# Four edits to a chain of expert and scan blocks: ranking by halves, scan weights requested a stage earlier, a changed order in the gated scan, and a first sequence with an order of its own

## The chip, the cores and the metric

One NeuronCore of one Trainium2 chip runs the whole program in one launch. The metric is the time of that launch on the device in microseconds (us). Names of engines in the profile: PE is TensorE, DVE is VectorE, ACT is ScalarE, POOL is GpSimd, and SP is SyncE, which here only issues DMAs.

## What is computed

The input is x of shape [8, 1024, 128] in f32: 8 sequences of 1024 tokens, 128 features. Six blocks follow each other, each reading a layer-normalised x and adding to x. Cut to what matters, the reference is:

```python
x = x + 0.5 * L0_ffn(layernorm(x))    # m0: 8 experts, the best two by logits, gated
x = x + L0_attn(layernorm(x))         # s0: gated scan
x = x + 0.5 * L0_ffn(layernorm(x))    # m1: as m0
x = x + 0.5 * L1_ffn(layernorm(x))    # m2: 8 experts, the best two by probabilities, capacity
x = x + L1_attn(layernorm(x))         # s1: selective scan
x = x + 0.5 * L1_ffn(layernorm(x))    # m3: as m2

# L0_ffn: logits = xn @ Wg + bg; the two largest, softmax over the two
#   y = (silu(xn @ W1a + b1a) * (xn @ W1b + b1b)) @ W2 + b2, summed by weight
# L1_ffn: probs = softmax(x @ router_w.T); the two largest, rank within the expert,
#   those beyond the capacity dropped; y = silu(x @ w1) @ w2, plus x
# L0_attn: xc, z = split(x @ W_in); u = silu(conv4(xc)); dt_raw, B = split(u @ W_x)
#   dt = clip(softplus(dt_raw @ W_dt + b_dt), 1e-4, 1); ub = u * (B @ W_Bp)
#   h[t] = h[t-1] * (1 - dt[t]) + ub[t]; y = (h + D * u) * silu(z); y @ W_out
# L1_attn: u = silu(conv4(x) + b); dt, B, C by head from u; delta = softplus(dt @ dtw + b)
#   s[t] = s[t-1] * exp(delta * A) + delta * u * B[t], for 16 states; y = sum(s * C) ...
```

## The kernel before

**Blocks.** The six blocks run one behind the other, each as one or more groups of engine programs with semaphores of its own; x (`x_res`, [128, 64, 128]: 64 tiles of 128 tokens) stays in SBUF.

**Experts (`moe`).** A block begins with ranking. The 64 tiles go in 16 groups of four (`NG` = 16): VectorE makes statistics (`statistics`, `spreads`, `scales`), ScalarE takes the root (`root`), normalises (`normalise`) and copies the rows turned by TensorE (`copy_out`); TensorE multiplies them with the gate (`logits`) into one PSUM tensor `lps` of 64 x 8 numbers per partition. When all 16 groups are there, VectorE works on [128, 64, 8] at a time: in m0 and m1 it adds the gate's bias (L337), in m2 and m3 it copies (L341), takes the maximum and the difference, has ScalarE make the exponential (L535), and divides. Then for the best and the second-best expert it takes the maximum, marks what is below, adds the index of the expert and takes the least (L354 to L362); `chosen` (L364) is what TensorE counts from. There follow ranks and runs, 16 groups of marks by which TensorE finds for each row of the sorted list its token (L495), and the block map (`bmap`, L442 to L449): for each of the 73 blocks of 128 rows the expert whose run it lies in. Before, every partition computes it for all 73 blocks: it compares 73 x 8 numbers (m0, m1) or 73 x 32 (m2, m3, where there are `S` = 4 rounds of runs) and sums them, and where there are rounds it takes 8 off three times. `source` (L456) is the list of tokens. SyncE, once it has issued the expert weights (`loads`), waits for the rows that it stored. The expert loop then runs over 71 blocks per kind of expert; the change doesn't touch it. Between blocks of the program the engines meet.

**Gated scan (`gated_scan`, L892 on).** The loop is over v, at each v of which the engines work on several sequences: TensorE projects sequence v+1 (`project_in`, `project_z`, `project_low`, `project_wide`), projects out v-1 (`project_out`) and turns the rows of v+2; ScalarE scales the fetched rows of v+3 (L1195), normalises v+2 (L1143), makes u by silu (L1163, L1179), and copies z (L1173) and xp (L1206); VectorE convolves half 0 of v+1 (L1263; half 1 is convolved on TensorE by four taps, L1067), adds the output of v-1 (L1239), makes statistics of v+2, scans v (L1278) and reads the wide projections (L1303, L1306). Eight PSUM banks go round in the order of one list, `order` (L955), so TensorE's order of blocks and the list are one. At its start SyncE issues the 16 loads of the weights (L989), then the fetches of rows (L1009); the engines wait for all loads.

**Selective scan (`selective_scan`, L1324 on).** For each of 8 sequences there are 2 halves x 16 states, 256 steps in all of 128 x 1024: ScalarE makes dA (L1694), POOL dBu (L1558), VectorE scans (L1873) and multiplies with C (L1880), TensorE sums. The work for sequence t = s + 1 is put in 32 slots i within the 32 steps of s; for t = 0 the slots run without steps, s = -1. Lists of slots say when each engine's `conv`, silu, `xd`, `dt`, exponential and logarithm stand. `soften` (L1536) is four operations on POOL: from the pieces of the softplus they make delta, and du = delta * u. SyncE stores the rows of B and C and loads them spread over the partitions.

## Time and profile before

| | us |
|---|---|
| median of 3 runs | 3280.31 |
| lowest, highest | 3279.01, 3280.53 |
| the execution that was profiled | 3282.22 |
| its span in the trace | 3279.4 |
| ranking of m0, m1, m2, m3 | 105.4, 103.5, 162.6, 121.6 |
| expert loops of m0, m1, m2, m3 | 410.4, 406.5, 277.3, 376.4 |
| gated scan | 285.9 |
| selective scan | 1017.5 |

The stages are cut at 12.3, 117.7, 528.1, 814.0, 917.5, 1324.0, 1486.6, 1763.9, 2781.4, 2903.0 and 3279.4 us of the span. In a timeline each row gives the start and the length in us, the engine, the line of the kernel, what is written from what, how many instructions of a kind the row gathers (its length then is that of all of them), and in brackets how long the engine was idle before it and which engine's or queue's event ended that. A window's row gives for each engine the busy time and the number of instructions in it, then TensorE's granted clock (1.00 is full speed) and the busy share of the DMA engines.

### The profile page before, as it was taken

The numbers are of one execution on the slowest core, as the hardware profiler recorded it, in microseconds if no ns is written. First come the engines' busy times: TensorE is split into PE (matmuls) and PEld (weight loads), VectorE is DVE, ScalarE is ACT, GpSimd is POOL, SyncE is SP. The second block draws the span as 40 slices with busy tenths as digits, with TensorE's granted clock in tenths as the row PEclk, the third lists the DMA queues.
The fourth block names the chain that finished last, engine by engine and source line by source line (L and its number), as shares of the span: only waits on it lengthen the run. The fifth ranks groups of instructions, "written<-read, shape, count | busy, mean of one in ns | idle before, by whom it ended". The sixth has DMA issues, their size and how long they took to land. (4 is left out here: it accounts for less than half of the span.)

```text
span 3279.4 us, 43901 instructions
## 1 busy us (share of the span) xinstructions
PE 2580.4 (79%) x12400; PEld 1850.5 (56%) x12400; DVE 2222.7 (68%) x3998; ACT 1575.7 (48%) x2668; POOL 2018.0 (62%) x1643
## 2 busy tenths in 40 slices
PE   5799994996689999348996678788877875579782
PEld 4599993443579999327995233333332322559672
DVE  5656663786766666683332699999999998653333
ACT  4433333884533333333333667567577662443330
POOL 0377771232057776305772789999999784335776
PEclk9999997998599999569998899999999999589997
DMA  6111112100411111422332689889888886312333
GB/s 180 32 48 48 46 48 56 39 26 1 135 37 48 46 47 40 134 72 61 87 87 43 243 291 310 278 296 305 285 291 301 288 300 207 103 40 76 92 90 85
DMA packets 287326, 429.78 MB, mean 131 GB/s; under 512 B 59196, under 2 KB 196799, under 8 KB 287200
## 3 DMA queue, kind: packets, MB, share of 16 engines
q1 hardware_dynamic: 251744, 357.54, 33.1%
q0 software_dynamic: 35456, 70.86, 9.3%
q8 instruction: 42, 0.69, 0.1%
q14 instruction: 84, 0.69, 0.1%
HBM read 367.71 MB, written 62.39 MB: 131 GB/s over the span
## 5 line engine op out<-in xcount | busy, mean ns | idle before, releaser
L683 POOL DMA_INDIRECT m_rows<-rows_in,m_source x568 | 554.0, 975 | 588.6 <-SPq L580 222.2
L1593 PE MATMUL s_y_ps<-s_prod,ident 128*128 128x512 f32 x1024 | 522.0, 634 | 214.3 <-DVE s_prod L1880 214.3
L1558 POOL TENSOR_TENSOR s_dBu<-s_du,s_B_row 128x1024 f32<-128x1024 f32 x256 | 602.4, 2359 | 84.6 <-DVE s_dA L1873 71.1
L1873 DVE TENSOR_TENSOR_SCAN s_dA<-s_dA,s_dBu 128x1024 f32<-128x1024 f32 x256 | 585.6, 2287 | 44.3 <-POOL s_dBu L1558 44.3
L721 PE MATMUL m_A_ps<-m_rowsT,m_own 128*128 128x256 f32 x2272 | 569.0, 383 | 2.1 <-ACT m_rowsT L763 1.1
L737 PE MATMUL m_Y_ps<-m_own,m_hid 128*128 128x128 f32 x4544 | 556.1, 276 | 3.6 <-issue 3.6
L737 PEld LDWEIGHTS m_Y_ps<-m_own,m_hid 128*128 128x128 f32 x4544 | 531.4, 192 | 5.7 <-issue 5.6
L1593 PEld LDWEIGHTS s_y_ps<-s_prod,ident 128*128 128x128 f32 x1024 | 180.9, 195 | 523.3 <-DVE s_prod L1880 325.9
L773 ACT ACTIVATE m_act_a<-m_A_ps,m_own 128x256 f32<-128x256 f32 x568 | 238.5, 471 | 434.7 <-PE m_A_ps L721 318.9
L721 PEld LDWEIGHTS m_A_ps<-m_rowsT,m_own 128*128 128x128 f32 x2272 | 414.9, 193 | 48.8 <-ACT m_rowsT L763 1.9
L1694 ACT ACTIVATE s_dA<-s_delta,s_decay 128x1024 f32<-128x1024 f32 x256 | 286.0, 1118 | 311.0 <-DVE s_prod L1880 306.2
L690 POOL DMA_INDIRECT rows_by_token<-m_y_sb,m_target x284 | 308.8, 1087 | 121.9 <-issue 90.6
L822 DVE SCALAR_TENSOR_TENSOR m_hid<-m_B_ps,m_own,m_act_a 128x256 f32<-128x256 f32 x568 | 247.2, 477 | 200.2 <-ACT m_act_a L773 183.5
L778 ACT ACTIVATE m_hid<-m_A_ps 128x512 f32<-128x512 f32 x284 | 169.7, 598 | 335.9 <-PE m_A_ps L721 335.9
L1880 DVE TENSOR_TENSOR s_prod<-s_dA,s_C_row 128x1024 f32<-128x1024 f32 x256 | 313.2, 1223 | 10.1 <-issue 1.4
L727 PE MATMUL m_B_ps<-m_rowsT,m_own 128*128 128x256 f32 x1136 | 293.4, 381 | 0.0
L836 DVE COPY m_y_sb<-m_Y_ps 128x256 f32<-128x256 f32 x142 | 60.3, 425 | 328.3 <-PE m_Y_ps L737 328.3
L727 PEld LDWEIGHTS m_B_ps<-m_rowsT,m_own 128*128 128x128 f32 x1136 | 217.3, 191 | 30.0
L805 DVE COPY m_own<-m_packs 128x1032 f32 (+1 forms) x284 | 172.7, 608 | 71.5 <-PE m_A_ps L721 47.2
L643 POOL DMA_INDIRECT m_mine<-rows_out,get x176 | 169.2, 961 | 59.1 <-issue 40.8
L715 PE MATMUL m_T_ps<-ident,m_rows 128*128 128x128 f32 x568 | 112.5, 280 | 81.2 <-DMA m_rows<-rows_in,m_source 81.2
L495 PE MATMUL m_src<-m_coded,m_is_low 128*128 128x284 bf16 x512 | 82.2, 307 | 101.3 <-ACT m_coded L538 101.3
(241 smaller groups left out, 3543.9 us busy)
## 6 DMA issues: line engine op xcount, KB each, us to landing
s_B_row<-s_bc_rows SPq DMA_DIRECT2D x256, 512.0 KB, 5.7
s_C_row<-s_bc_rows SPq DMA_DIRECT2D x256, 512.0 KB, 6.0
rows_out<-m_y_sb SPq DMA_DIRECT2D x142, 128.0 KB
rows_in<-m_xs SPq DMA_DIRECT2D x64, 256.0 KB, 2.3
m_rows<-rows_in,m_source POOLq DMA_INDIRECT x568
s_got<-rows_by_token SPq DMA_DIRECT2D x16, 512.0 KB, 5.0
m_got<-rows_by_token SPq DMA_DIRECT2D x32, 256.0 KB, 3.9
rows_by_token<-m_y_sb,m_target POOLq DMA_INDIRECT x284
```

The costliest lines, as they stand in the source:

```text
L683: pool.indirect_dma_start(rows[:, b % AHEAD, r, :], None, c.rows_in, bass.IndirectOffsetOnAxis(source[:, 2 * b + r:2 * b + r + 1], 0)).the ...
L690: pool.indirect_dma_start(c.rows_by_token, bass.IndirectOffsetOnAxis(target[:, 2 * b + r:2 * b + r + 1], 0), y_sb[:, b % AHEAD, r, :], Non ...
L721: ins = nc.tensor.matmul(A_ps[h][:, j, :], own[:, slot, W1A + f * P:W1A + (f + 1) * P], rowsT[:, slot, :], start=True, stop=True)
L727: ins = nc.tensor.matmul(B_ps[h][:, j, :], own[:, slot, W1B + f * P:W1B + (f + 1) * P], rowsT[:, slot, :], start=True, stop=True)
L737: ins = nc.tensor.matmul(Y_ps[slot][:, r, :], hid[:, slot, f, at(r, P)], own[:, slot, W2 + f * D:W2 + (f + 1) * D], start=(f == 0), stop=( ...
L773: ins = nc.scalar.activation(act_a[:, h, j, :], A_ps[h][:, j, :], ACT.Silu, bias=own[:, slot, B1A + f:B1A + f + 1])
L822: ins = nc.vector.scalar_tensor_tensor(out=hid[:, slot, f, :], in0=B_ps[h][:, j, :], scalar=own[:, slot, B1B + f:B1B + f + 1], in1=act_a[: ...
L1558: nc.gpsimd.tensor_tensor(dBu[q % RING][:, :], du[s % 2][:, h, :], B_row[q % RING][:, :], ALU.mult).then_inc(dBu_ready, 1)
L1593: ins = nc.tensor.matmul(y_ps[:, at(cc, 512)], c.ident[:, :], prod[q % 2][:, at(cc, 512)], start=(n == 0), stop=(n == NS - 1))
L1694: nc.scalar.activation(dA[q % 2][:, :], delta[s % 2][:, h, :], ACT.Exp, scale=decay[:, h, n:n + 1]).then_inc(dA_ready, 1)
L1873: nc.vector.tensor_tensor_scan(dA[q % 2][:, :], dA[q % 2][:, :], dBu[q % RING][:, :], 0.0, ALU.mult, ALU.add).then_inc(scanned, 1)
L1880: nc.vector.tensor_tensor(prod[q % 2][:, :], dA[q % 2][:, :], C_row[q % RING][:, :], ALU.mult).then_inc(prod_ready, 1)
```

## The change

**Ranking.** `lps` becomes two PSUM tensors, and the operations on [128, 64, 8] become two of [128, 32, 8]. The first half runs when eight of 16 groups have their logits. In m2 and m3 its copy, maximum and difference stand ahead of the statistics of group 14, and its exponential ahead of the normalising of that group.

```diff
+                def softmax(part, step):
+                    ts = at(part, NT // 2)
+                    if step == 0:
+                        dve.wait_ge(logits_done, (part + 1) * NG // 2)
+                        link(nc.vector.tensor_copy(L[:, ts, :], lps3[part]))
+                        link(nc.vector.tensor_reduce(m[0][:, ts], L[:, ts, :], AX.X, ALU.max))
+                        nc.vector.tensor_tensor(t8[:, ts, :], L[:, ts, :], over_experts(m[0][:, ts]), ALU.subtract).then_inc(logits_shifted, 1)
+                    else:
+                        dve.wait_ge(exp_done, part + 1)
+                        link(nc.vector.tensor_reduce(ind[:, ts], u8[:, ts, :], AX.X, ALU.add))
+                        link(nc.vector.reciprocal(rank[:, ts], ind[:, ts]))
+                        link(nc.vector.tensor_tensor(L[:, ts, :], u8[:, ts, :], over_experts(rank[:, ts]), ALU.mult))
+
+                def best_two(part):
+                    ts = at(part, NT // 2)
+                    for k in range(2):
+                        link(nc.vector.tensor_reduce(m[k][:, ts], L[:, ts, :], AX.X, ALU.max))
+                        link(nc.vector.tensor_tensor(t8[:, ts, :], L[:, ts, :], over_experts(m[k][:, ts]), ALU.is_lt))
+                        link(nc.vector.scalar_tensor_tensor(out=t8[:, ts, :], in0=t8[:, ts, :], scalar=float(E),
+                                                            in1=c.expert_id[:, ts, :], op0=ALU.mult, op1=ALU.add))
+                        link(nc.vector.tensor_reduce(ind[:, ts], t8[:, ts, :], AX.X, ALU.min))
+                        link(nc.vector.tensor_tensor(oh[k][:, ts, :], c.expert_id[:, ts, :], over_experts(ind[:, ts]), ALU.is_equal))
+                        if k == 0:
+                            link(nc.vector.scalar_tensor_tensor(out=L[:, ts, :], in0=oh[0][:, ts, :], scalar=-3e38,
+                                                                in1=L[:, ts, :], op0=ALU.mult, op1=ALU.add))
+
                 for g in range(NG):
                     if rows_before:
                         add_rows(g)
                     if g % 2 == 0 and g > 0:
                         scales(g // 2 - 1)
+                    if g == NG - 2 and not gated:
+                        softmax(0, 0)
                     statistics(g)
                     if g % 2 == 1:
                         spreads(g // 2)
...
+                for part in range(2):
+                    if gated:
+                        dve.wait_ge(logits_done, (part + 1) * NG // 2)
+                        link(nc.vector.tensor_tensor(L[:, at(part, NT // 2), :], lps3[part],
+                                                     gate_b[:, :].unsqueeze(1).to_broadcast([P, NT // 2, E]), ALU.add))
+                    else:
+                        if part == 1:
+                            softmax(1, 0)
+                        softmax(part, 1)
+                    best_two(part)
```

The same operations on the whole tensors, which stood behind the wait for all 16 groups, are gone.

**Block map.** `block_row` is one number per partition (128 times the partition), so partition p computes for block p only; a diagonal matrix of the result is multiplied by ones on TensorE, and the row copied out of `tot_ps`.

```diff
+                link(nc.vector.tensor_scalar(passed[:, :], run_end[:, :, :].rearrange("p i e -> p (i e)"), c.block_row[:, 0:1], None, ALU.is_le))
+                link(nc.vector.tensor_reduce(bmap[:, :], passed[:, :], AX.X, ALU.add))
+                link(nc.vector.tensor_copy(bmap_i[:, :], bmap[:, :]))
+                link(nc.vector.tensor_scalar(bmap_i[:, :], bmap_i[:, :], E - 1, None, ALU.bitwise_and))
+                link(nc.vector.tensor_copy(bmap[:, :], bmap_i[:, :]))
+                nc.vector.tensor_scalar(spread_map[:, :], c.ident[:, :], bmap[:, 0:1], None, ALU.mult).then_inc(map_ready, 1)
...
                 link(nc.vector.tensor_tensor(source[:, :], code, second, ALU.add))
+                dve.wait_ge(map_spread, 1)
+                link(nc.vector.tensor_copy(block_pack[:, :], tot_ps[:, 0:NBLK + 2]))
...
+                pe.wait_ge(map_ready, 1)
+                nc.tensor.matmul(tot_ps[:, 0:P], c.ones_bf[:, :], spread_map[:, :], start=True, stop=True).then_inc(map_spread, 1)
```

The exponential on ScalarE (lines as in the changed kernel), of the block m2:

```diff
+                def exponentials(part):
+                    act.wait_ge(logits_shifted, part + 1)
+                    nc.scalar.activation(u8[:, at(part, NT // 2), :], t8[:, at(part, NT // 2), :], ACT.Exp).then_inc(exp_done, 1)
+
...
+                        exponentials(0)
                     normalise(g)
                     if g > 0:
                         copy_out(g - 1)
                 copy_out(NG - 1)
-                act.wait_ge(logits_shifted, 1)
                 if gated:
```

ScalarE's order in block m2 between the root of the last pair of groups (L504 before, L521 now) and the exponential (L535, L542). Names: `m_xs` normalised rows, `m_xcT` turned rows, `m_u` exponentials. Before:

```order
L504 ACTIVATE m_spread<-m_spread 128x8
L512 ACTIVATE m_xs<-x_res,m_shift,m_rstd 128x128 x4
L521 COPY m_xcT<-m_tps 128x512
L512 ACTIVATE m_xs<-x_res,m_shift,m_rstd 128x128 x4
L521 COPY m_xcT<-m_tps 128x512 x2
L535 ACT_TABLE_LOAD
L535 ACTIVATE m_u<-m_t 128x512
```

Now:

```order
L521 ACTIVATE m_spread<-m_spread 128x8
L542 ACT_TABLE_LOAD
L542 ACTIVATE m_u<-m_t 128x256
L529 ACTIVATE m_xs<-x_res,m_shift,m_rstd 128x128 x4
L538 COPY m_xcT<-m_tps 128x512
L529 ACTIVATE m_xs<-x_res,m_shift,m_rstd 128x128 x4
L538 COPY m_xcT<-m_tps 128x512 x2
L542 ACTIVATE m_u<-m_t 128x256
```

The table load and half of the exponential now stand ahead of the last eight rows of `m_xs`; the second half stays behind the copies, without a load.

**Weights.** Each scan's weight tensors are allocated outside both stages, so that they live through m0 (m2) as well. POOL clears two of them at the start of that block's ranking, and SyncE issues the 16 loads there.

```diff
+                if ahead is not None:
+                    ahead.request(sp)
...
+    def request(sp):
+        def load(dst, src, **kw):
+            sp.dma_start(dst, src, **kw).then_inc(weights.loaded, 16)
+        load(weights.w_in[:, :], w["w_in"])
+        load(weights.tap_rows[:, :, :], w["taps"].rearrange("(a k) i -> a k i", a=1).to_broadcast([P, CONV, INNER]))
...
+        for h in range(HALVES):
+            load(weights.w_x[:, h, :, :], w["w_x"][at(h, P), :].unsqueeze(1).to_broadcast([P, COPIES, PAIR]))
+        sp.wait_ge(weights.zeroed, 2)
+        for r in range(COPIES):
+            load(weights.w_dt[r * PAIR:r * PAIR + PAIR // 2, :], w["w_dt"])
+            load(weights.w_b[r * PAIR + PAIR // 2:r * PAIR + PAIR, :], w["w_b"])
+    weights.clear, weights.request = clear, request
```

The loads themselves are those removed from the scans' programs; SyncE's program of the gated scan now begins with the fetch of rows.

**Gated scan.** TensorE's blocks and the list of banks change order, `y` gets a second buffer, and VectorE adds the output behind the scan.

```diff
         order = []
         for v in range(-3, SEQS + 1):
-            for s, uses in ((v + 1, (("in", range(N_DVE)),)), (v - 1, (("out", range(2)),)),
-                            (v + 1, (("in", range(N_DVE, HALVES * HC)), ("z", range(HALVES * HC)), ("low", range(HC)),
-                                     ("wide", range(HALVES * HC)))),
+            for s, uses in ((v + 1, (("in", range(HALVES * HC)), ("z", range(HALVES * HC)), ("low", range(HC)))),
+                            (v - 1, (("out", range(2)),)), (v + 1, (("wide", range(HALVES * HC)),)),
                             (v + 2, (("turned", range(2)),)), (v + 1, (("wide", range(HALVES * HC, 2 * HALVES * HC)),)),
                             (v + 3, (("sum", range(4)),))):
...
                 if has(v + 1):
-                    project_in(v + 1, range(N_DVE))
+                    project_in(v + 1, range(HALVES * HC))
+                    project_z(v + 1)
+                    project_low(v + 1)
                 if has(v - 1):
                     project_out(v - 1)
                 if has(v + 1):
-                    project_in(v + 1, range(N_DVE, HALVES * HC))
-                    project_z(v + 1)
-                    project_low(v + 1)
                     project_wide(v + 1, 0)
                 if has(v + 2):
...
-                if s > 0:
+                if s > 1:
                     for g in range(2):
-                        Use("out", s - 1, g).read(dve)
+                        Use("out", s - 2, g).read(dve)
...
                 if has(v + 1):
                     convolve(v + 1)
-                if has(v - 1):
-                    add_out(v - 1)
                 if has(v + 2):
                     statistics(v + 2)
                 if has(v):
                     scan(v)
+                if has(v - 1):
+                    add_out(v - 1)
                 if has(v + 1):
                     widened(v + 1)
```

TensorE's order of one period of the gated scan; names: `s_w_in` with `s_xnT` the projections in (L1071, L1162) and z (L1079, L1170), `s_w_conv` the four taps, `s_w_out` the projection out, `s_w_x` low, `s_w_dt` and `s_w_b` wide, `ident` the turned rows. Before:

```order
L1071 MATMUL s_bank<-s_xnT,s_w_in 128x512 x2
L1054 MATMUL s_bank<-s_w_out,s_y 128x128 x16
L1067 MATMUL s_bank<-s_xnT,s_w_conv 128x512 x8
L1079 MATMUL s_bank<-s_xnT,s_w_in 128x512 x4
L1098 MATMUL s_bank<-s_u,s_w_x 128x512 x4
L1108 MATMUL s_bank<-s_xp,s_w_dt 128x512 x4
L1089 MATMUL s_bank<-ident,s_xn 128x128 x8
```

Now:

```order
L1162 MATMUL s_bank<-s_xnT,s_w_in 128x512 x2
L1158 MATMUL s_bank<-s_xnT,s_w_conv 128x512 x8
L1170 MATMUL s_bank<-s_xnT,s_w_in 128x512 x4
L1189 MATMUL s_bank<-s_u,s_w_x 128x512 x4
L1145 MATMUL s_bank<-s_w_out,s_y 128x128 x16
L1199 MATMUL s_bank<-s_xp,s_w_dt 128x512 x4
L1180 MATMUL s_bank<-ident,s_xn 128x128 x8
```

The sixteen matmuls of the projection out went from behind the first two of `s_w_in` to between low and the wide dt.

**Selective scan, first sequence.** Half 0 goes through ahead of half 1, on TensorE and ScalarE; VectorE softens half 0 in place of POOL; B and C rows of half 0 are stored and loaded from slot 16, those of half 1 from slot 26. du of a half waits for u of that half alone.

```diff
+                if t == 0:
+                    for h in range(HALVES):
+                        order += [(role, 0, h * HC + cc) for role in ("conv", "xd", "dt") for cc in range(HC)]
+                else:
+                    order += [("conv", t, k) for k in range(3)] + [("xd", t, 0), ("xd", t, 1), ("conv", t, 3)]
+                    order += [("dt", t, 0), ("dt", t, 1), ("xd", t, 2), ("xd", t, 3), ("dt", t, 2), ("dt", t, 3)]
             if EARLY <= t + 1 < SEQS:
...
+                if t == 0:
+                    if i == 16:
+                        store_bc(0, (0,))
+                        sp.wait_ge(bc_stored, 16)
                         for q in range(RING):
                             load_B(q)
                             load_C(q)
-                if s == -1 and i == ALLN - 1:
-                    for q in range(RING, RING + 2):
-                        load_B(q)
-            sp.wait_ge(loaded, LOADS)
+                    if i == 26:
...
+                if s == -1:
+                    XD_AT, DT_AT = (13, 14, 21, 22), (15, 16, 23, 24)
+                    CONV_AT = (9, 10, 11, 12, 17, 18, 19, 20)
...
+                if s == -1:
+                    CONV_AT, SILU_AT, XD_AT, DT_AT = (11, 12, 21, 22), (13, 23), (14, 15, 24, 25), (16, 17, 27, 28)
+                    EXP_AT, LOG_AT, ROUNDED_AT = (18, 29), 19, 20
                 if 0 <= s < SEQS:
...
+                if s == -1 and 26 <= i < 30:
+                    soften_on(dve, nc.vector, 0, 0, i - 26)
```

ScalarE's order there; `s_u` is u, `s_xd` the low projection, `s_e` and `s_delta` the two forms of dt. Before:

```order
L1726 ACTIVATE s_u<-s_bank,s_conv_b 128x512 x2
L1743 ACT_TABLE_LOAD
L1743 ACTIVATE s_u<-s_u 128x1024
L1726 ACTIVATE s_u<-s_bank,s_conv_b 128x512
L1752 COPY s_xd<-s_bank 96x512 x2
L1726 ACTIVATE s_u<-s_bank,s_conv_b 128x512
L1743 ACTIVATE s_u<-s_u 128x1024
L1760 ACTIVATE s_e<-s_bank,s_dt_b 128x512
L1761 ACTIVATE s_delta<-s_bank,s_dt_b 128x512
```

Now:

```order
L1806 ACTIVATE s_u<-s_bank,s_conv_b 128x512 x2
L1823 ACT_TABLE_LOAD
L1823 ACTIVATE s_u<-s_u 128x1024
L1832 COPY s_xd<-s_bank 96x512 x2
L1840 ACTIVATE s_e<-s_bank,s_dt_b 128x512
L1841 ACTIVATE s_delta<-s_bank,s_dt_b 128x512
L1840 ACTIVATE s_e<-s_bank,s_dt_b 128x512
L1841 ACTIVATE s_delta<-s_bank,s_dt_b 128x512
L1846 ACT_TABLE_LOAD
L1846 ACTIVATE s_e<-s_e 128x1024
```

The copies of xd and the dt of half 0 now stand directly behind its silu, with its exponential's table load next; conv and silu of half 1 went behind them.

## Rows read from the trace of the kernel before

**Rows 1.** Busy time of each engine in two stages (columns as named)

```profile
1324.00:1486.60 162.60, 63.03 (x322) 51.78 (x322) 131.40 (x420) 58.60 (x108) 31.60 (x64) 0.59 0.36 104
...
1763.90:2781.40 1017.50, 775.46 (x1856) 314.94 (x1856) 940.00 (x714) 631.18 (x745) 843.94 (x431) 0.94 0.81 275
```

**Rows 2.** The same view, one period of the gated scan

```profile
644.70:673.57 28.87, 27.02 (x93) 14.17 (x92) 25.12 (x42) 23.87 (x45) 10.19 (x4) 1.00 0.14 37
```

**Rows 3.** Timeline, gated scan's start: start, length, engine, line, operation, count, [idle before]

```profile
528.09 0.34 SPq L989 DMA_DIRECT2D s_w_in<-in_L_attn_W_in  x1
...
537.52 1.05 SPq L1009 DMA_DIRECT2D s_got<-rows_by_token  x2
...
544.71 0.37 ACT L1195 ACTIVATE s_bank<-s_got,weight 128x128 f32<-128x128 f32 x1 [32.93 <-DMA s_got<-rows_by_token]
```

**Rows 4.** Timeline, VectorE, selective scan's start and its first scan

```profile
1775.31 1.43 DVE L1902 TENSOR_TENSOR s_w_conv<-s_e 128x256 f32<-128x256 f32 x4 [15.72 <-DMA s_w_dt<-in_dt_proj_T]
...
1830.39 2.30 DVE L1873 TENSOR_TENSOR_SCAN s_dA<-s_dA,s_dBu 128x1024 f32<-128x1024 f32 x1 [44.31 <-POOL s_dBu L1558]
```

**Rows 5.** Timeline, VectorE, ranking of block m0

```profile
61.16 0.69 DVE L337 TENSOR_TENSOR m_L<-m_lps,m_gate_b 128x512 f32<-128x512 f32 x1 [8.66 <-PE m_lps L476]
...
69.85 0.69 DVE L364 TENSOR_TENSOR m_chosen<-m_oh 128x512 bf16<-128x512 f32 x1
```

**Rows 6.** Groups of instructions by line and shape: 256 elements on VectorE

```profile
L832 DVE TENSOR_TENSOR m_y_sb<-m_Y_ps,m_own_b 128x256 f32<-128x256 f32 x142 | 60.3, 425 | 106.5 <-PE m_Y_ps L737 106.5
```

**Rows 7.** Timeline, end of ranking in block m1

```profile
912.57 1.19 PE L495 MATMUL m_src<-m_coded,m_is_low 128*128 128x284 bf16 x8 [0.73 <-ACT m_coded L538]
...
914.15 0.31 DVE L452 TENSOR_SCALAR m_found<-m_src 128x142 f32<-128x142 f32 x1
```

**Rows 8.** Timeline, first sequence of the selective scan, ScalarE and POOL

```profile
1796.90 1.28 ACT L1743 ACT_TABLE_LOAD   x1
1798.19 1.06 ACT L1743 ACTIVATE s_u<-s_u 128x1024 f32<-128x1024 f32 x1
...
1806.69 0.67 ACT L1760 ACTIVATE s_e<-s_bank,s_dt_b 128x512 f32<-128x512 f32 x1
...
1818.18 2.34 POOL L1537 TENSOR_TENSOR s_e<-s_e 128x1024 f32<-128x1024 f32 x1 [36.42 <-ACT s_e L1777]
```

**Rows 9.** Timeline, ranking of block m2, ScalarE and VectorE

```profile
1402.63 1.65 ACT L512 ACTIVATE m_xs<-x_res,m_shift,m_rstd 128x128 f32<-128x128 f32 x4 [0.62 <-DVE m_own_shift L319]
...
1411.26 0.69 DVE L341 COPY m_L<-m_lps 128x512 f32<-128x512 f32 x1 [8.66 <-PE m_lps L476]
...
1424.08 0.69 DVE L364 TENSOR_TENSOR m_chosen<-m_oh 128x512 bf16<-128x512 f32 x1
```

**Rows 10.** Timeline, ScalarE, ranking of block m3

```profile
2819.89 1.65 ACT L512 ACTIVATE m_xs<-x_res,m_shift,m_rstd 128x128 f32<-128x128 f32 x4 [0.62 <-DVE m_own_shift L319]
```

**Rows 11.** Timeline, VectorE, block map of block m2

```profile
1476.90 2.59 DVE L442 TENSOR_TENSOR m_passed<-block_row,m_run_end 128x2336 f32<-128x2336 f32 x1
...
1483.90 0.31 DVE L452 TENSOR_SCALAR m_found<-m_src 128x142 f32<-128x142 f32 x1
```

**Rows 12.** Timeline, one period of the gated scan, TensorE and ScalarE

```profile
660.30 3.59 PE L1098 MATMUL s_bank<-s_u,s_w_x 128*128 128x512 f32 x8
665.75 3.67 PE L1108 MATMUL s_bank<-s_xp,s_w_dt 128*128 128x512 f32 x8 [1.85 <-ACT s_xp L1206]
...
657.61 1.07 ACT L1163 ACTIVATE s_u<-s_bank 128x512 f32<-128x512 f32 x2
...
661.52 3.18 ACT L1143 ACTIVATE s_xn<-x_res,s_shift,s_rstd 128x128 f32<-128x128 f32 x8 [0.42 <-POOL s_shift L1024]
664.61 1.04 ACT L1206 COPY s_xp<-s_bank 128x512 f32<-128x512 f32 x2
```

**Rows 13.** Timeline, TensorE, an earlier period of the gated scan

```profile
601.82 5.40 PE L1098 MATMUL s_bank<-s_u,s_w_x 128*128 128x512 f32 x8 [1.86 <-ACTq L1166]
```

**Rows 14.** The page's costliest groups: 1024 elements on VectorE

```profile
L1880 DVE TENSOR_TENSOR s_prod<-s_dA,s_C_row 128x1024 f32<-128x1024 f32 x256 | 313.2, 1223 | 10.1 <-issue 1.4
```

356 lines of the change are left out of this document (181 added, 175 removed).

## The prediction

> **What bounds the kernel now.** I read the page first, then the busy times by stage, then timelines around each edited place. The execution that was profiled took 3282.22 us, of which 3279.4 are its span. The median of the runs shown is 3280.31, 1.9 less, so whatever I work out for the profiled execution is laid on the median with that shift. No engine bounds the whole: in the selective scan VectorE is busy 940.0 of 1017.5 us [rows 1], in the expert loops TensorE is, and in between lie stretches where the engines wait for each other once per stage. The change touches three such stretches (ranking, the start of each scan, the first sequence of the selective scan) and one loop, the gated scan, where TensorE is busy 27.02 of each 28.87 us, VectorE 25.12 and ScalarE 23.87 [rows 2]. So each edit is read at its place, for what ends last there.
>
> **Weights a stage ahead.** In the gated scan SyncE issues 16 loads before the first rows; the first is issued at 528.09 and the fetch of rows follows at 537.52. ScalarE starts to scale those rows at 544.71, 7.2 us after the fetch [rows 3]. With the loads gone the fetch stands at 528.1, ScalarE starts at 535.3: **-9.4 us**. VectorE's products of the convolution weights and its scalings then run at once, under the fetch's 7 us. In the selective scan the stage begins at 1763.9 and VectorE and ScalarE wait for the last load until 1775.31 [rows 1, 4]; nothing else is waited for, since x is in SBUF: **-11.4 us**. The loads don't vanish: 16 issues of together 9 us go to SyncE behind that routing block's own weight loads, ahead of its waits for the stored rows, and their cover is the ranking that runs then (SyncE has nothing to store or fetch until it ends; the stage of m2 lasts 162.6 us with its DMA engines busy 36% [rows 1]). If the cover were gone, 9 us would come back in each.
>
> **Ranking by halves, gated blocks (m0, m1).** From the last logits VectorE runs 12 operations of 512 elements, 61.16 to 69.85, a pitch of 0.724 and 0.69 for one; before them it sat idle 8.66 us [rows 5]. A 256-element operation takes 0.42 [rows 6]; with the same 0.035 between two I take 0.46. Behind the last logits now stand 12 half operations, 5.5 us instead of 8.69: -3.2 each. The other half (5.5) fits in the idle of 8.66. Two blocks: **-6.4**. The block map's two operations of 584 elements (0.8 each) make way for six small ones, a matmul and a copy; the source table that follows starts at 914.15, when TensorE's last group of marks (912.57 plus 1.19) ends [rows 7], so the saving stops at that matmul: 0.
>
> **The same in m2 and m3.** There the first half begins before the last statistics: three half operations on VectorE (3 x 0.46 = 1.4 us), then on ScalarE the exponential with its table load (1.28 as in [rows 8], plus 0.4) before the last two groups are normalised. In m2 VectorE runs without a gap up to ScalarE's normalising at 1402.63 [rows 9] and hands on its 1.4 us; with ScalarE's share, less the 0.62 that ScalarE waits there, I get 2.5 us for the last logits, so the copy of the logits moves from 1411.26 to 1413.7. Behind it: 1.4 (copy, maximum, difference), 0.4 (exponential), 1.3 (sum, reciprocal, product), 11 x 0.46 = 5.1, to 1421.9, against 1424.08 [rows 9]: -2.2. In m3 VectorE waits for ScalarE there, its 1.4 us fit, and only ScalarE's 1.7 less its wait of 0.62 counts, 1.1 us [rows 10]: -3.7. The block map is 2336 elements wide here: its first operation takes 2.59 and the whole, from 1476.90 to the next table at 1483.90, 7.0 us [rows 11]. In its place come six operations on 32, 1 and 128 elements and a copy of 73, each at or below the 0.31 that 142 elements take [rows 7]; at 0.22 to 0.28 they are 1.6 us: **-5.4 each**, since VectorE alone sets this tail and the matmul that spreads the map runs under the source table's five operations. Both blocks: -2.2 - 3.7 - 10.8 = **-16.7**.
>
> A table load in this trace is followed by its activation after 1.29 us (1796.90, then 1798.19) [rows 8]. The Trainium skill ("ScalarE: Activation LUTs", What ACT_TABLE_LOAD costs) has about 1380 ns of drain on top for each switch; here that would be 1.4 more in m2, in m3 and for the extra switch in the selective scan, and a total of about -42 instead of -46. The row shows none of it, and I leave it out.
>
> **The gated scan's loop.** TensorE's order changes from in, out, in (four taps), z, low, wide to in, in, z, low, out, wide. Its only gap is 1.85 us before the wide dt at 665.75, waiting for ScalarE's copy of xp (664.61 plus 1.04) [rows 12]. Behind z the low projection needs ScalarE's u, which ends at 657.61 + 1.07 = 658.68 after ScalarE has run from the turned copy without a gap. Now low could start at 658.8 and not 660.30: low 3.43, out 3.57, wide dt at 665.8, where it stood at 665.75. So the gap moves from before the wide dt to before low (some 2 us) and the period stays: **0 for some six periods**. The ends between which this lies: ScalarE's own round leaves 0.42 (before 661.52 [rows 12]) and 0.16, so if out did not stand in the way the gain would be 0.6 a period, -3.5; if the whole gap closed, -11. The other end is TensorE's clock: a low block of eight that takes 3.59 took 5.40 at 601.82, behind a gap of 1.86, in this scan [rows 12, 13]. If each new gap brought that, 6 x 1.8 = +11. I take 0, because the arithmetic of the long round leaves it at +0.02, and the old gap was as long as the new one. The output's addition on VectorE moves behind the scan, where it fits before the wide dt; the second buffer of y keeps it off the scan.
>
> **First sequence of the selective scan.** From silu of half 0 (ends 1799.25) the old chain runs over ScalarE, then four POOL operations of 2.34 from 1818.18, then dBu, to the first scan at 1830.39 [rows 4, 8]. Now half 0 runs through alone: xd and dt on TensorE and ScalarE to 1804.9, exponential, logarithm and rounding with two tables 6.9 (to 1811.8), softening on VectorE in four operations of 1.22 (the shape of [rows 14]) to 1816.9, dBu 2.4 more. What ends last then is ScalarE: before the first decay it must also do all of half 1 (conv, a table and silu, xd, dt, a table and exponential). By rows that is, from 1799.25 on, 12 evacuations of xd and dt at a pitch of 0.57, 2 of conv at 0.6, 4 tables at 1.29, 6 activations of 1024 elements at 1.06 and the rounding at 1.15 [rows 8], together 20.7 us, and I count 4.6 of waiting for TensorE (its xd and dt blocks of 1.1 to 1.8 us stand between ScalarE's): the decay starts at 1824.6, the first scan at 1825.7, -4.7. With TensorE at its lower clock behind the new gaps, half as much again or more as in [rows 13], it is 1830 or so. **Taken -2.5, bounds -4.7 and +0.5.** The 256 steps behind it keep their pitch of 3.46, which is VectorE's scan and product.
>
> **Sum.** -9.4 - 11.4 - 6.4 - 16.7 + 0 - 2.5 = **-46.4**; 3282.2 - 46.4 = 3235.8 profiled, and 3280.3 - 46.4 = **3234** as a median.
>
> **The rivals.**
> (a) The gated scan's periods lengthen by the clock. For it: 601.82, and a routing stage with gaps that is granted 0.59 of the clock [rows 1, 13]; against it: in the period shown the clock was 1.00 although it held a gap of 1.85 [rows 2, 12]. +11: 3245.
> (b) The periods shorten, because the out block fills time and the output's addition no longer stands ahead of the statistics. For it: 0.58 of slack on ScalarE; against it: out stands between low and the wide dt. -3.5 to -11: 3223 to 3230.
> (c) The first sequence gives nothing, or the halves in m2 and m3 give only what the block map does: +2.5 or +5.9, 3237 to 3240.
> (d) The change does not do what it says: the loads, issued among a routing block's traffic, hold up its rows, or the first halves run late and stand before the last statistics. Losing one scan's load and half of the ranking gives 3254.
> (e) **Slower.** TensorE at half clock through the whole run from the new gap: low, out and wide dt, 3.43 + 3.57 + 3.51 = 10.5 us of work that ends last, in each period. That costs +10.5 x 6 = 63, and the total is 3297, +17. It decides from 8.8 us lost per period on (53 us), since below that the 46 saved and the 6.6 of the bound hold. The row of 601.82 shows 1.8 lost, not 8.8.
>
> **How the numbers follow.** The forecast with (c), which ends within its bounds: 0.66, of which 0.10 for (c). (a) 0.15, (b) 0.12, (d) 0.06, (e) 0.01. The forecast's own bounds are 3229 to 3241. To leave out no more than 2 in 10 the range takes (a) and most of (b): **3222 to 3250**. About 0.2% (6.6 us) is what a measurement can tell from no change. Cases (a) to (d) all end more than that below, though (d) could be heavier than I price it: faster 0.98, same 0.01, slower 0.01.
>
> **What would show each step.** In the trace after: no loads at the scans' starts and the first scaling of rows near 535 in the gated scan; VectorE's first product in the selective scan within 1 us of its stage's start. From the copy of the logits to the chosen mask 5.5 us in m0 and m1, and 8.2 in m2 and m3, the exponential's table ahead of the last two groups. Block map: the source table follows the last marks by under 3 us in m2. In the gated scan a period of 28.9 with TensorE's gap before low, and its clock near 1.00. The first scan of the selective scan 66.5 - 11.4 - 2.5 = 52.6 us behind its stage's start (50.4 to 55.6 by the bounds). I would be wrong if periods of the gated scan are not within 0.5 us of 28.9, if ScalarE's waits in the first sequence are much over 4.5, or if VectorE waits for the logits longer than before by more than 2.5 us in m2.

## The result, and the profile after

The changed kernel took 3239.4 us as the median of four runs (3234.7, 3235.5, 3243.3, 3244.0) against 3280.4 before: a ratio of 0.9875, 95% interval 0.9857 to 0.9894, or -41.0 us. The forecast was 3234 in a range from 3222 to 3250. The direction and most of the size are right; most of the 5 us on top comes from one step, and the runs are 9 us apart where those before lay within 2. The profiled execution is the slowest of the four, 3244.02 with a span of 3241.7.

Timeline of the kernel after, ranking of m0 on VectorE (the row of the second half's first operation, and `chosen`), against [rows 5]:

```profile
61.20 0.42 DVE L370 TENSOR_TENSOR m_L<-m_lps,m_gate_b 128x256 f32<-128x256 f32 x1 [3.15 <-PE m_lps L491]
...
66.69 0.69 DVE L379 TENSOR_TENSOR m_chosen<-m_oh 128x512 bf16<-128x512 f32 x1
```

Twelve operations of 0.42 in place of 0.69, `chosen` 3.2 earlier. The wait for the logits shrank from 8.66 to 3.15 us because the first half lies in it.

Block m2, ScalarE and VectorE, against [rows 9, 11]: the table load ahead of the normalising, the copy of the last logits, `chosen`, then the new block map up to the copy of its row.

```profile
1397.05 1.28 ACT L542 ACT_TABLE_LOAD   x1
...
1398.66 1.63 ACT L529 ACTIVATE m_xs<-x_res,m_shift,m_rstd 128x128 f32<-128x128 f32 x4
```

```profile
1387.58 2.31 DVE L293 SCALAR_TENSOR_TENSOR x_res<-m_got,weight,x_res 128x128 f32<-128x128 f32 x8 [1.74 <-DMA m_got<-rows_by_token]
...
1407.23 0.42 DVE L333 COPY m_L<-m_lps 128x256 f32<-128x256 f32 x1 [1.59 <-PE m_lps L491]
...
1415.38 0.69 DVE L379 TENSOR_TENSOR m_chosen<-m_oh 128x512 bf16<-128x512 f32 x1
```

```profile
1468.18 0.24 DVE L457 TENSOR_SCALAR m_passed<-m_run_end,block_row 128x32 f32<-128x32 f32 x1
...
1469.45 0.30 DVE L465 TENSOR_SCALAR m_found<-m_src 128x142 f32<-128x142 f32 x1
...
1471.00 0.24 DVE L471 CAST m_block_pack<-m_tot 128x73 int32<-128x73 f32 x1
```

From the copy to `chosen` 8.15 us, where it was 12.8; from the start of the block map to the next table 1.27 us, where it was 7.0.

The gated scan's start, SyncE and ScalarE, against [rows 3]:

```profile
524.07 12.89 SPq L1102 DMA_DIRECT2D s_got<-rows_by_token  x4
```

```profile
531.11 4.77 ACT L1285 ACTIVATE s_bank<-s_got,weight 128x128 f32<-128x128 f32 x16 [23.36 <-DMA s_got<-rows_by_token]
```

And one of its periods on TensorE (low, out, wide dt), with the window of that period, against [rows 2, 12]:

```profile
678.96 5.40 PE L1189 MATMUL s_bank<-s_u,s_w_x 128*128 128x512 f32 x8 [1.87 <-ACTq L1256]
684.19 3.73 PE L1145 MATMUL s_bank<-s_w_out,s_y 128*128 128x128 f32 x32
687.76 3.60 PE L1199 MATMUL s_bank<-s_xp,s_w_dt 128*128 128x512 f32 x8
```

```profile
664.90:695.51 30.61, 28.74 (x94) 14.75 (x92) 25.30 (x42) 23.62 (x45) 10.20 (x4) 0.94 0.13 35
```

Low takes 5.40 us where it took 3.59, the granted clock of the period is 0.94 and the period is 30.61 us long, not 28.87. Once, in the first period, it is the wide dt that is slow:

```profile
566.10 5.37 PE L1199 MATMUL s_bank<-s_xp,s_w_dt 128*128 128x512 f32 x8 [1.96 <-ACT s_xp L1296]
```

The selective scan's first sequence on POOL, VectorE and ScalarE, against [rows 4, 8]:

```profile
1754.78 1.67 POOL L1622 TENSOR_TENSOR s_rstd<-s_spread,s_minus_half 128x8 f32<-128x8 f32 x1 [4.35 <-DVE s_shift L1936]
```

```profile
1786.50 1.23 DVE L1535 TENSOR_TENSOR s_e<-s_e 128x1024 f32<-128x1024 f32 x1 [31.88 <-ACT s_e L1857]
...
1803.69 2.30 DVE L1957 TENSOR_TENSOR_SCAN s_dA<-s_dA,s_dBu 128x1024 f32<-128x1024 f32 x1 [9.59 <-ACT s_dA L1774]
```

```profile
1792.52 0.58 ACT L1832 COPY s_xd<-s_bank 96x512 f32<-96x512 f32 x1 [2.11 <-PE s_bank L1724]
...
1796.23 0.69 ACT L1840 ACTIVATE s_e<-s_bank,s_dt_b 128x512 f32<-128x512 f32 x1 [1.42 <-PE s_bank L1732]
```

The softening runs on VectorE from 1786.50 at 1.23 an operation, and the first scan now waits for ScalarE's decay and not for POOL.

### The profile page after: what moved, and what is told of

Same layout as the page of the kernel before. It is cut to its first block and busy times, and to the rows that moved or that the text cites. A ratio compares the mean times of both kernels' runs of the same rounds, so it can differ in the third digit from the quotient of the medians.

```text
span 3241.7 us, 43980 instructions
## 1 busy us (share of the span) xinstructions
PE 2599.9 (80%) x12404; PEld 1861.5 (57%) x12404; DVE 2220.8 (69%) x4064; ACT 1577.1 (49%) x2671; POOL 2016.9 (62%) x1639
## 5 line engine op out<-in xcount | busy, mean ns | idle before, releaser
L717 POOL DMA_INDIRECT rows_by_token<-m_y_sb,m_target x284 | 317.0, 1116 | 114.4 <-issue 85.2
L832 DVE COPY m_own<-m_packs 128x1032 f32 (+1 forms) x284 | 164.8, 580 | 74.1 <-PE m_A_ps L748 43.9
```

Source lines behind the costliest of these rows:

```text
L717: pool.indirect_dma_start(c.rows_by_token, bass.IndirectOffsetOnAxis(target[:, 2 * b + r:2 * b + r + 1], 0), y_sb[:, b % AHEAD, r, :], Non ...
```

## The two traces side by side

Each line is the same stretch in both profiled executions, from the start of one instruction to the start of another; the source table is the operation that writes `m_source`.

| stretch | before | after | difference | predicted |
|---|---|---|---|---|
| start of the span to `chosen` in m0 | 69.85 | 66.69 | -3.2 | -3.2 |
| gated scan, first instruction to the first scaled rows | 16.6 | 7.0 | -9.6 | -9.4 |
| gated scan, fetch of rows to the first stored rows of m1 | 282.9 | 292.1 | +9.2 | 0 |
| m1, first stored rows to its source table | 94.9 | 91.5 | -3.5 | -3.2 |
| m2, last wait for rows to `chosen` | 30.3 | 27.8 | -2.5 | -2.2 |
| m2, `chosen` to the source table | 61.0 | 55.3 | -5.8 | -5.4 |
| m2, source table to the selective scan's first power on POOL | 294.7 | 284.1 | -10.6 | -11.4 |
| from there to the first scan | 50.6 | 48.9 | -1.7 | -2.5 |
| m3, first statistics to `chosen` | 60.1 | 56.2 | -3.9 | -3.7 |
| m3, `chosen` to the source table | 61.0 | 55.3 | -5.8 | -5.4 |

Seven of ten are within 0.4 us of the forecast and two within 0.8. Together they are -37.4, and the span fell by 37.7. The stretches between them, the expert loops and the fetches of rows, differ by some 2 us from execution to execution (the last wait for rows in m2 came 65.7 us after the stage's first fetch before, 67.5 after, and between 66.9 and 68.7 in the twelve other traces; the kernel before has the shortest of all, and whether a part of these 2 us belongs to the change is not shown). What has to be explained is +9.2 in the gated scan.

## The experiments

Three theories to begin with. Theory 1 is rival (a) of the prediction: the gap of 1.87 us that now stands ahead of low brings TensorE to its lower level (1.2 GHz) in some periods, and 1.7 to 1.8 us are lost in each. Theory 2: the spread of the runs comes from elsewhere, the DMAs of the expert loops. Theory 3: the new order itself makes the period longer. Times are compared with the kernel before on the same chip. The first four kernels ran where that takes 3279.0 us, the other eight where it takes 3523.6 and 3525.0; where those 245 us are, the last section says.

| kernel | median, us | runs | against before |
|---|---|---|---|
| again (the changed kernel) | 3238.3 | 3232.6 to 3242.7 | -40.8 |
| old_order | 3234.8 | 3234.0 to 3235.8 | -44.3 |
| filled_gap | 3244.1 | 3242.6 to 3244.9 | -34.9 |
| split_out | 3227.4 | 3225.2 to 3228.3 | -51.6 |
| filled_two | 3483.1 | 3478.7 to 3486.9 | -40.5 |
| out_first | 3476.1 | 3467.2 to 3482.2 | -47.5 |
| weights_only | 3503.3 | 3502.9 to 3508.7 | -20.3 |
| ranking_only | 3500.7 | 3497.0 to 3503.2 | -22.9 |
| split_again | 3480.5 | 3477.3 to 3483.1 | -44.5 |
| split_old_first | 3475.2 | 3473.9 to 3476.7 | -49.7 |
| split_fed | 3471.9 | 3467.1 to 3474.4 | -53.0 |
| split_mid | 3474.8 | 3473.0 to 3478.9 | -50.1 |

### again: the changed kernel once more

> The changed kernel once more, unchanged, in more rounds. Its four runs so far lie in two groups, 3234.7 and 3235.5 against 3243.3 and 3244.0, and the profiled one, of the upper group, has periods of 30.6 us in the gated scan with the low block at 5.40 us behind the new gap. Theory 1 (TensorE's clock, my rival a): two groups again, 8 to 9 us apart, since the lower clock behind the gap sets in in some executions and then returns every period; a profile of the lower group would show periods of 28.9 and low at 3.6. Theory 2 (the two groups come from something else, DMA latencies of the expert loops): a spread without two groups, or both groups with periods of 30.6.

Not two groups but a spread, 3232.6, 3237.1, 3239.4 and 3242.7. The profiled run (3237.1) shows both kinds of period in one execution. TensorE's low block in two neighbouring periods, then the windows of these periods (engines as named, then TensorE's granted clock):

```profile
675.36 5.40 PE L1189 MATMUL s_bank<-s_u,s_w_x 128*128 128x512 f32 x8 [1.86 <-ACTq L1256]
...
705.96 3.70 PE L1189 MATMUL s_bank<-s_u,s_w_x 128*128 128x512 f32 x8 [1.86 <-ACTq L1256]
```

```profile
661.30:691.91 30.61, 28.75 (x94) 14.78 (x92) 25.30 (x42) 23.62 (x45) 10.20 (x4) 0.94 0.13 35
691.91:720.80 28.89, 27.03 (x93) 14.18 (x92) 25.18 (x42) 23.59 (x45) 10.20 (x4) 1.00 0.14 37
```

Both wait 1.86 us ahead of low. Behind the first the clock is at its lower level and the period takes 30.61 us; behind the second it isn't and the period takes 28.89. The two windows hold the same work. A period that is hit loses 1.7 us (5.40 against the 3.70 that low takes behind a gap when the clock stays up). In the trace of the changed kernel five low blocks take 5.40 and one wide dt 5.37; in this one three low blocks take 5.40. The first of the three, in the loop's second period, costs nothing. Low and the wide dt there in again, and then in ranking_only (the kernel before with the new ranking), where low was not hit:

```profile
587.79 5.40 PE L1189 MATMUL s_bank<-s_u,s_w_x 128*128 128x512 f32 x8 [1.86 <-ACTq L1256]
593.97 3.67 PE L1199 MATMUL s_bank<-s_xp,s_w_dt 128*128 128x512 f32 x8 [0.79 <-ACT s_xp L1296]
```

```profile
657.08 3.70 PE L1125 MATMUL s_bank<-s_u,s_w_x 128*128 128x512 f32 x8 [1.86 <-ACTq L1193]
663.26 3.67 PE L1135 MATMUL s_bank<-s_xp,s_w_dt 128*128 128x512 f32 x8 [2.48 <-ACT s_xp L1233]
```

No block out stands between the two in this period, the wide dt waits for ScalarE's xp, and it starts 6.18 us behind low either way. So six stretches cost time in the one execution and two in the other, 4 x 1.7 = 6.8 us apart. The stretch of the table above is 292.1 and 285.4 us, 6.7 apart, and the executions are 3244.0 and 3237.1. Without any hit both loops would take some 282.0 us, 0.9 less than the kernel before: the +9.2 of the table is six hits, 10.2 us, less 1. Theory 1 holds, and theory 2 falls for this difference, since it lies in the loop. That the executions fall into two groups was wrong: it is the number of periods that is hit.

### old_order: the loop as before

```diff
-            for s, uses in ((v + 1, (("in", range(HALVES * HC)), ("z", range(HALVES * HC)), ("low", range(HC)))),
-                            (v - 1, (("out", range(2)),)), (v + 1, (("wide", range(HALVES * HC)),)),
+            for s, uses in ((v + 1, (("in", range(N_DVE)),)), (v - 1, (("out", range(2)),)),
+                            (v + 1, (("in", range(N_DVE, HALVES * HC)), ("z", range(HALVES * HC)), ("low", range(HC)),
+                                     ("wide", range(HALVES * HC)))),
...
-                if has(v - 1):
-                    add_out(v - 1)      # behind scan(v)
+                if has(v - 1):
+                    add_out(v - 1)      # ahead of statistics(v + 2)
```

(`project_in`, `project_z`, `project_low` and `project_out` on TensorE alike)

> The changed kernel with the gated scan's order as before (TensorE's blocks, the list of banks, the output's addition on VectorE); y keeps its second buffer. Theory 1: periods of 28.9, no second group, 3234 to 3236. Theory 2: the two groups stay, 3235 and 3243.

3234.8 with runs 1.8 us apart, 282.6 us for the loop. The low block and the wide dt, with TensorE's wait behind low again:

```profile
589.01 5.40 PE L1190 MATMUL s_bank<-s_u,s_w_x 128*128 128x512 f32 x8 [1.86 <-ACTq L1258]
...
676.70 3.60 PE L1190 MATMUL s_bank<-s_u,s_w_x 128*128 128x512 f32 x8
682.14 3.67 PE L1200 MATMUL s_bank<-s_xp,s_w_dt 128*128 128x512 f32 x8 [1.84 <-ACT s_xp L1298]
```

The first row is the scan's second period, in which the fill of the pipeline still leaves low waiting: it takes 5.40 behind a gap of 1.86, as at 601.82 before [rows 13]. In the six periods behind it low has no gap and takes 3.60; in five of them the gap ahead of the wide dt is as long (1.84, once 2.21), and the block behind it takes 3.67. The same holds for all 20 such gaps in the four traces with the old order (before, old_order, weights_only, ranking_only), while in after and again the 1.86 ahead of low was followed by the lower level in seven of ten such periods. The place alone is no rule: in the loop's first period the wide dt took 5.37 behind waits of 1.91 to 2.38 in after, weights_only, split_again and split_mid, and low in the second period took 5.40 in six of twelve traces. So the new order of the gated scan, which the prediction valued at 0, costs 3.5 us in the median and up to 9 in one execution, though the fastest runs of the changed kernel (3232.6, 3234.7) are no slower than old_order. Of the parts it is the only one that cost time on this chip. The other parts give -44.3 together; predicted were -46.4.

### filled_gap and filled_two: work that nobody needs in the gap

```diff
+                Use("low", t, 0).fill(pe)
+                for _ in range(4):      # filled_two: range(2)
+                    nc.tensor.matmul(Use("low", t, 0).ps[:, :], w_in[:, 0:P], w_in[:, :], start=True, stop=True)
                 pe.wait_ge(u_ready, t * HALVES + HALVES)
```

> The changed kernel with four more matmuls (each 128x512, 0.43 us) ahead of TensorE's wait for u before low, into the bank that low then overwrites, so the gap of 1.87 us is filled with work that nobody needs. Theory 1: no lower clock, low at 3.6, periods 28.9, one group at 3234 to 3236 although TensorE does 14 us more. Theory 3 (the period is longer by the order itself, not by the clock): 3243 or more in all runs.

> As filled_gap, with two surplus matmuls in place of four: the profile of filled_gap shows that four took 3.44 us and not 1.7, twice what I had written, so they reached 1.6 us beyond the gap of 1.87 and made the periods 30.2 without any lower clock. Two take 1.72 and end inside the gap. Theory 1 (the clock): periods 28.9, low at 3.6 in all of them, runs within 2 us of each other at 3232 to 3235. Theory 3 (the order itself is slower): 3237 or more, spread as the changed kernel.

Four matmuls were sized wrongly: an f32 matmul of 512 columns takes 0.86 us and not 0.43 (the profile counts each as two). TensorE in one period of filled_gap, then of filled_two:

```profile
677.12 3.60 PE L1186 MATMUL s_bank<-s_w_in 128*128 128x512 f32 x8
680.56 3.60 PE L1193 MATMUL s_bank<-s_u,s_w_x 128*128 128x512 f32 x8
```

```profile
675.20 1.88 PE L1186 MATMUL s_bank<-s_w_in 128*128 128x512 f32 x4
677.23 3.70 PE L1193 MATMUL s_bank<-s_u,s_w_x 128*128 128x512 f32 x8 [0.16 <-ACTq L1260]
```

In filled_gap the surplus ends 1.6 us after u is there and the period is 30.21 long, with the clock up:

```profile
661.66:691.87 30.21, 30.21 (x102) 15.78 (x101) 25.28 (x42) 23.61 (x45) 10.20 (x4) 1.00 0.12 36
```

The loss there is work, not clock. In filled_two the surplus takes 1.88 and low, 0.16 behind it, 3.70; from the end of z at 675.20 the period is 28.9 long. The loop takes 284.3 us, with one lower stretch of the clock left in it (at the wide dt at 653.82, 5.20 us), against 282.6 to 283.5 in four traces with the old order. So the order itself costs 1 us at most, and theory 3 falls. By its runs alone filled_two would not show this: -40.5 is 3238.5 where the first chip takes 3279.0, and theory 1 had said 3232 to 3235. The runs still lie in two pairs, 3479 and 3487, which this does not explain; the first sequence below is the place in which its profile stands out.

### split_out and out_first: where out should stand

```diff
-                    project_z(v + 1)
-                    project_low(v + 1)
-                if has(v - 1):
-                    project_out(v - 1)
+                    project_z(v + 1)
+                if has(v - 1):
+                    project_out(v - 1, 0)
+                if has(v + 1):
+                    project_low(v + 1)
+                if has(v - 1):
+                    project_out(v - 1, 1)
```

(and the list of banks alike; out_first has both parts ahead of low)

> The changed kernel with the projection out in two parts: the first group (1.8 us) between z and low, where TensorE waits for u, the second between low and the wide dt. From the rows before: z ends, out 1.8, low starts when u is there, low 3.43, out 1.8, and the wide dt then waits for xp, which ScalarE has 0.6 earlier. Theory 1: no gap of more than 1.4, the clock stays, periods 28.2 to 28.9, 3230 to 3236 in one group. Theory 3: no better than the changed kernel's upper group.

> The changed kernel with the whole projection out between z and low. split_out was 7 us faster than the old order, with periods of 28.1 where TensorE waits 0.74 for xp. Theory 4 (what shortens the period is that ScalarE has xp 0.6 us earlier, because the output's addition no longer stands ahead of the statistics on VectorE, and that low, out and wide no longer stand in one row behind u): also 28.1 to 28.3 here, 3227 to 3230, with a gap of 1.1 to 1.4 before the wide dt. Theory 5 (the split itself does it, by removing the long gap): the period of the old order, 28.9, and 3233 to 3235.

TensorE in one period of split_out (out, low, out, wide dt), then of out_first (out, low, wide dt):

```profile
670.45 1.95 PE L1145 MATMUL s_bank<-s_w_out,s_y 128*128 128x128 f32 x16
672.47 3.70 PE L1189 MATMUL s_bank<-s_u,s_w_x 128*128 128x512 f32 x8
676.01 1.95 PE L1145 MATMUL s_bank<-s_w_out,s_y 128*128 128x128 f32 x16
678.70 3.67 PE L1199 MATMUL s_bank<-s_xp,s_w_dt 128*128 128x512 f32 x8 [0.74 <-ACT s_xp L1299]
```

```profile
675.10 3.73 PE L1145 MATMUL s_bank<-s_w_out,s_y 128*128 128x128 f32 x32
678.67 3.60 PE L1189 MATMUL s_bank<-s_u,s_w_x 128*128 128x512 f32 x8
683.36 3.67 PE L1199 MATMUL s_bank<-s_xp,s_w_dt 128*128 128x512 f32 x8 [1.10 <-ACT s_xp L1296]
```

Both have periods of 28.1 (the wide dt stands at 655.25 and 683.36 in out_first), with waits of 0.74 and 1.10 ahead of the wide dt, and loops of 276.4 and 277.8 us, 5 to 6 below the old order. So the split is not what does it (theory 5 falls). ScalarE's z and normalising in old_order, then in out_first:

```profile
675.23 2.27 ACT L1265 ACTIVATE s_z<-s_bank 128x512 f32<-128x512 f32 x4 [0.16 <-ACT s_u L1255]
677.91 3.19 ACT L1235 ACTIVATE s_xn<-x_res,s_shift,s_rstd 128x128 f32<-128x128 f32 x8 [0.41 <-POOL s_shift L1116]
```

```profile
677.20 2.07 ACT L1263 ACTIVATE s_z<-s_bank 128x512 f32<-128x512 f32 x4 [0.16 <-ACT s_u L1253]
679.13 3.19 ACT L1233 ACTIVATE s_xn<-x_res,s_shift,s_rstd 128x128 f32<-128x128 f32 x8
```

From the start of z to that of the normalising it takes 2.7 us with the output's addition ahead of the statistics, the last 0.41 waiting for POOL's shift, and 1.9 with the addition behind the scan. It is 1.9 in the changed kernel too (679.03 to 680.96), where all of out stands between low and the wide dt, and in split_out (672.55 to 674.47). So ScalarE has xp 0.7 earlier, and that shortens the period as soon as not all of out stands between low and the wide dt. (That the addition's place alone does this was not run; the rows say it.) The prediction had this 0.58 of ScalarE as rival (b) and held that out stood in the way; it does, but only because of its place. split_out is faster than both kernels: 3227.4 against 3239.4 and 3280.4. Its period of 28.1 is a little below the expected 28.2 to 28.9, out_first's is what was expected; but out_first's -47.5 (3231.5 where the first chip takes 3279.0) misses the 3227 to 3230, with runs 15 us apart.

### weights_only and ranking_only: the other parts alone

> The kernel before with the scans' weights requested a stage ahead and nothing else (y in two buffers, which the loop's order doesn't use). Predicted -9.4 and -11.4, so 3279.0 - 20.8 = 3258.2, and 3256 to 3260 if the requests stay hidden behind the ranking; over 3265 if they hold up the rankings' rows or the expert loops' first weights.

> The kernel before with the ranking by halves and the new block map and nothing else. Predicted -23.1, so 3255.9; by the trace of the changed kernel m2 gave some 1.5 less than predicted, so 3256 to 3258. If the four parts take from each other (a shared cover), the two single parts would sum to more than the 44.3 us by which old_order is faster than the kernel before.

-20.3 and -22.9, where -20.8 and -23.1 were predicted. They sum to -43.2. That old_order, which has the new first sequence in addition, is at -44.3 (on the other chip) leaves some -1 for it, less than the 6 us by which the runs of either kernel differ.

### The first sequence of the selective scan

split_out was 7.3 us faster than old_order, though its loop is only 6.2 shorter, and filled_two's runs are in two pairs. The way from POOL's first power to the first scan differs: 50.6 in the order before (also in weights_only and ranking_only), 48.9 to 49.1 in after, again, old_order and filled_gap, 45.4 in split_out, 53.7 and 53.8 in filled_two and out_first. Four kernels on one chip, all with the loop of split_out:

```diff
 # split_old_first: the whole selective scan in the order before, weights ahead
 # split_fed, in project_x, ahead of the wait for u
+                if t == 0 and cc == 0:
+                    for _ in range(3):
+                        nc.tensor.matmul(use.ps[:, :], w_z[:, 0:P], w_conv[:, 0:2, :].rearrange("p k i -> p (k i)"), start=True, stop=True)
 # split_mid, for t = 0 (and the lists of slots)
+                    order += [("conv", 0, k) for k in range(3)] + [(role, 0, cc) for role in ("xd", "dt") for cc in range(HC)]
+                    order += [("conv", 0, 3)] + [(role, 0, HC + cc) for role in ("xd", "dt") for cc in range(HC)]
```

> split_out once more, as the base of the three kernels beside it. So far the way from POOL's first power (s_rstd) of the selective scan to its first scan was 50.6 us in the order before, and with the new first sequence 48.9 to 49.1 in four profiles, 45.4 in split_out and 53.7 in two profiles of the slower chip. Theory 6 (TensorE's clock in the first sequence: where its lower stretches fall decides between 45.4 and 53.7): again one of these values, and runs that differ by steps of 4 to 8 us.

> split_again with the selective scan's first sequence in the order before. Theory 6: 50.6 us to the first scan here, whatever the state, and runs closer together than those of split_again; against it the new order is worth -5.2, -1.6 or +3.1 in one execution, by the clock. Theory 7 (the new order is worth a constant 1.6): slower by 1.6 with the same spread.

> split_again with three surplus matmuls (128x512, 0.86 each at full clock) ahead of each of the two waits for u in the first sequence, where TensorE waits 3.2 us for silu; xd overwrites what they write. Theory 6: TensorE's gaps shrink to 0.6 and the clock stays up through xd and dt, some 45.4 us or less to the first scan; where the clock is low already they take 5.2 and cost 2 each. If the lower clock has nothing to do with these gaps: 49 or 54 as before, plus up to 4.

> split_again with the conv of half 1's first 512 columns put ahead of xd of half 0 on TensorE and ScalarE (conv 0, 1, 2, xd 0, 1, dt 0, 1, conv 3, xd 2, 3, dt 2, 3), useful work in the first gap of 3.2 us. It takes 3.4 at full clock, 0.2 beyond the gap, and 0.6 on ScalarE. Theory 6: the clock stays up, 45 to 46.5 us to the first scan. Theory 7: 49.0 plus 0.6 or so.

Measured to the first scan: 53.5, 50.2, 45.8 and 47.9 us. TensorE's xd and dt of half 0, and xd of half 1, in split_again, in split_fed (behind its surplus), and in split_mid, where xd and dt of half 0 stand directly behind three convs and xd of half 1 behind a wait of 7.4:

```profile
1936.66 3.73 PE L1727 MATMUL s_bank<-s_u,s_w_xd 128*96 128x512 f32 x4 [3.20 <-ACT s_u L1826]
1940.32 3.78 PE L1735 MATMUL s_bank<-s_xd,s_w_dt 32*128 32x512 f32 x4
...
1957.01 3.73 PE L1727 MATMUL s_bank<-s_u,s_w_xd 128*96 128x512 f32 x4 [3.20 <-ACT s_u L1826]
```

```profile
1934.32 2.74 PE L1728 MATMUL s_bank<-s_w_conv,s_w_z 128*128 128x512 f32 x6
1937.69 1.96 PE L1730 MATMUL s_bank<-s_u,s_w_xd 128*96 128x512 f32 x4 [0.63 <-ACT s_u L1829]
1939.57 1.98 PE L1738 MATMUL s_bank<-s_xd,s_w_dt 32*128 32x512 f32 x4
...
1954.15 1.96 PE L1730 MATMUL s_bank<-s_u,s_w_xd 128*96 128x512 f32 x4 [0.52 <-ACT s_u L1829]
```

```profile
1938.42 2.10 PE L1727 MATMUL s_bank<-s_u,s_w_xd 128*96 128x512 f32 x4
1940.45 1.98 PE L1735 MATMUL s_bank<-s_xd,s_w_dt 32*128 32x512 f32 x4
...
1954.09 3.73 PE L1727 MATMUL s_bank<-s_u,s_w_xd 128*96 128x512 f32 x4 [7.40 <-ACT s_u L1826]
```

xd and dt take 3.73 and 3.78 at the lower level, 1.96 and 1.98 at the upper one, and both halves' blocks stand in the chain. With work in the two waits of 3.2 us they stay at the upper level, and 7.7 us are gained over split_again by matmuls that compute nothing. (From the silu of half 0 to the first decay ScalarE waits 4.1 us for TensorE in split_out and 7.3 in after, so the prediction's 4.6 was right for the upper level only.) split_mid gains 5.6 of that with useful work in the first wait alone; xd of half 1 still stands behind a wait and takes 3.73, so it misses the 45 to 46.5 that were expected. The old order has the third conv in that place: xd of half 0 stands behind it without a wait and takes 2.10 in before, ranking_only and split_old_first. The way there is 50.2 to 50.6 in all four traces, although xd of half 1 takes 3.2 to 3.6 in these three; that it stays even because only half 0 is in the chain is read from the rows, not tested. So theory 6 holds for what decides the length. That the new order is worth a constant 1.6 (theory 7) falls: it is worth -5.2 where the clock is up (split_out), -1.7 where the blocks of one half are hit (after, again), and +3.3 where those of both are (split_again), and on this chip the old first sequence is the faster one, 3475.2 against 3480.5 (in the profiles 2.1 of that lie in the gated scan, where split_again's clock fell once). Why both halves are hit in all three traces of that order on this chip (filled_two, out_first, split_again), and one or none on the other, is open. The runs' spread was not explained to the end either: split_fed has 3467 to 3474 though its first sequence ought to hold.

## Why the prediction came out as it did

**Right.** The starts of the two scans (-9.4, -11.4: -9.6 and -10.6 by the traces, -20.3 by a kernel that has nothing else), for the reason given: the load was what ended last there, and at its new place it costs nothing that can be seen. The ranking (-23.1: -22.9 alone). The bound from the 256-element row held (0.42, pitch 0.457), the block map in m0 and m1 gave nothing because the last matmul of marks ended last, and in m2 and m3 it gave 5.8 less 0.3 for the copy. The last logits of m2 came 2.2 later behind their rows, where I had 2.5.

**Wrong: "I take 0" for the gated scan's loop.** The arithmetic of the round was right: without the clock the period is 28.89 (again), as worked out. The step that failed is the reason given against rival (a), that "the old gap was as long as the new one". It was, 1.85 against 1.87, but the old gap stood ahead of the wide dt, where old_order shows 1.84 with the clock up, and a gap of 1.86 ahead of low was followed by the lower level in five periods of the profiled execution. So the length of a gap did not say what it would cost. Two of the signs of being wrong that the prediction named came true: periods more than 0.5 us from 28.9, and, for the first sequence, waits of ScalarE well over 4.5 (7.3). I had read [rows 13] as an exception. It was the one period before in which low, and not only the wide dt, had to wait for ScalarE, so the only row that showed the new arrangement, and it showed the lower clock. It could not show the price: there the wide dt waits for xp behind low, and the 1.7 us vanish in that wait; with out between low and the wide dt they are lost in full. By that row's length the term is 6 x 1.8 = +11, by the median it was +3.5 (old_order against again) and by the profiled execution +9.2; taking the middle of 0 and +11 would have put the total at 3239.

**Mis-sized: the first sequence.** -2.5 taken, -1.7 measured, inside the bounds in this trace. But the bounds (-4.7 and +0.5) held one clock state for the whole and do not reach the +3.3 of split_again: with the xd and dt blocks of both halves at the lower level, the loss is 2 x 3.6 us of TensorE against the best case, and the convs ahead of them take 0.9 more (9.60 against 8.67 in split_out).

**Not seen.** That the addition of the output behind the scan was worth 0.7 a period, had out been put elsewhere. It stood in the prediction as slack of ScalarE and as a rival; which order of TensorE would collect it was not asked. The statement on table loads was right: 1397.05 to 1398.34, 1.29 us, and no drain behind it. The 1380 ns of drain for each switch that the Trainium skill states ("ScalarE: Activation LUTs", What ACT_TABLE_LOAD costs) do not show behind a load in any trace here.
